# Performer stage: feature products by four heads, over 64 rows and 256 columns, in place of six heads over 96 rows and 384 columns

## The reference, cut to what matters

```
h   = layernorm(x) * g + b                        # 32 x 87 x 192
qkv = h as 12 heads of 16 channels                # queries, keys and values are the same
u   = (qkv / 16**0.25) @ proj.T                   # proj 64 x 16: 64 features a head
q_p = exp(u - diag - max over the features of u) + 1e-4
k_p = exp(u - diag - max over tokens and features of u) + 1e-4
out = (q_p @ (k_p.T @ qkv)) / (q_p @ sum over tokens of k_p)
x   = x + out
```

## Time and profile before

| | us |
|---|---|
| median of three runs | 2725.62 (2723.99 to 2726.18) |
| the profiled execution | 2753.35 |
| its span | 2751.6 |
| of it the stages: choosing, to about | 70 |
| the Performer stage, from the first product of features to the last row added | 78.4 to 349.3 |
| mean granted clock of TensorE | 0.752 of full |

### The profile page before, as it was taken

The page is one execution under the profiler, slowest core; times in us unless marked ns, Lnnn a source line. Parts: engine busy times, 40 slices in busy tenths (PEclk is TensorE's granted clock), DMA queues, the critical chain, the costliest instruction groups (busy, mean ns, idle before and its releaser), DMA issues. The chain is left out here.

```text
span 2751.6 us, 36305 instructions
## 1 busy us (share of the span) xinstructions
PE 1749.3 (64%) x11724; PEld 1429.1 (52%) x11724; DVE 1481.6 (54%) x2882; ACT 1128.2 (41%) x2242; POOL 333.7 (12%) x402
## 2 busy tenths in 40 slices
PE   3688869566413777645995623323966598429993
PEld 2466749365312444524892422222854498329993
DVE  6588841521277999675224599997143300562223
ACT  5366743212144687721123288872324054102220
POOL 0000000046300000000330000000000143013441
PEclk9688869789855888855996855555985599569996
DMA  3100000234400000003761000000020253316774
GB/s 81 54 17 16 21 10 1 73 87 128 137 6 3 6 6 3 2 9 102 227 194 53 3 6 5 5 1 0 1 67 18 80 183 125 119 48 220 223 222 140
DMA packets 135104, 185.74 MB, mean 68 GB/s; under 512 B 49248, under 2 KB 110115, under 8 KB 134803
## 3 DMA queue, kind: packets, MB, share of 16 engines
q1 hardware_dynamic: 117015, 146.70, 17.3%
q0 software_dynamic: 15360, 35.05, 4.6%
q10 hardware_dynamic: 2556, 1.77, 0.3%
HBM read 148.35 MB, written 32.96 MB: 66 GB/s over the span
## 5 line engine op out<-in xcount | busy, mean ns | idle before, releaser
L917 DVE TENSOR_TENSOR 49_l3f_mlp_hidden<-49_l3f_mlp_gate,49_l3f_mlp_first 128x512 f32<-128x512 f32 x51 | 35.1, 688 | 189.0 <-ACT 49_l3f_mlp_gate L898 165.3
L2054 PE MATMUL 14_pla_line<-14_pla_low,ident 128*128 128x435 f32 x96 | 68.0, 875 | 62.0 <-ACT 14_pla_low L2102 62.0
L813 PE MATMUL 49_l3f_mlp_first<-49_l3f_mlp_xT,49_l3f_mlp_w 128*128 128x128 f32 x816 | 101.1, 278 | 0.0
L2254 PE MATMUL 30_log_int_turned<-identb,30_log_int_ratio 128*87 128x128 bf16 x272 | 32.7, 315 | 107.3 <-DVE 30_log_int_ratio L2772 107.3
L1124 PE MATMUL 2_performer_p_u<-perf_proj,2_performer_yT 96*87 96x384 f32 x204 | 94.4, 613 | 9.2 <-DVE 2_performer_arg L1286 8.0
L813 PEld LDWEIGHTS 49_l3f_mlp_first<-49_l3f_mlp_xT,49_l3f_mlp_w 128*128 128x128 f32 x816 | 96.9, 195 | 0.0
L933 DVE TENSOR_SCALAR 9_l0f_mlp_y<-9_l0f_mlp_second,l0f_routing_weight 128x192 f32<-128x192 f32 x51 | 21.3, 418 | 138.9 <-PE 9_l0f_mlp_second L827 71.2
L898 ACT ACTIVATE 49_l3f_mlp_gate<-49_l3f_mlp_first 128x512 f32<-128x512 f32 x51 | 30.5, 598 | 134.8 <-PE 49_l3f_mlp_first L818 134.8
L2254 PEld LDWEIGHTS 30_log_int_turned<-identb,30_log_int_ratio 128*87 128x87 bf16 x272 | 29.2, 194 | 108.9 <-DVE 30_log_int_ratio L2772 108.9
L2265 PE MATMUL 30_log_int_p_out<-l2a_vb,30_log_int_wT 87*87 87x16 bf16 x384 | 30.9, 222 | 83.4 <-ACT 30_log_int_wT L2694 83.4
L931 DVE TENSOR_TENSOR 42_l3a_mlp_y<-42_l3a_mlp_second,l3a_experts_b_rows 128x192 f32<-128x192 f32 x29 | 10.4, 358 | 134.8 <-PE 42_l3a_mlp_second L827 115.5
(11 more groups left out here) (888 smaller groups left out, 5376.9 us busy)
## 6 DMA issues: line engine op xcount, KB each, us to landing
49_l3f_mlp_w<-in_L_ffn_w_dram SPq DMA_DIRECT2D x51, 768.0 KB
26_l1f_mlp_w<-in_L_ffn_w_dram SPq DMA_DIRECT2D x29, 768.0 KB
42_l3a_mlp_w<-in_L_attn_W_dram SPq DMA_DIRECT2D x29, 576.0 KB
9_l0f_mlp_w<-in_L_ffn_down_w_dram SPq DMA_DIRECT2D x102, 96.0 KB
l3a_experts_w<-in_L_attn_W_dram SPq DMA_DIRECT2D x8, 576.0 KB, 8.2
14_pla_blocks<-l1a_qkb SPq DMA_DIRECT2D x192, 5.4 KB, 1.8
l1f_experts_w<-in_L_ffn_w_dram SPq DMA_DIRECT2D x8, 384.0 KB, 6.6
30_log_int_blocks<-l2a_qkb SPq DMA_DIRECT2D x192, 5.4 KB, 1.8
```

Source lines behind the costliest of these rows:

```text
L813: nc.tensor.matmul(to(t + a * PAIRS), of[:, t + a * PAIRS, :], at[:, 0, :], start=(t == 0), stop=True, skip_group_check=True)
L917: v.tensor_tensor(hidden[j % 2][:], gate[j % 2][:], first[j % 2][1][:, 0, 0:HT, :], ALU.mult).then_inc(hidden_done, 1)
L2054: nc.tensor.matmul(to_w[:, n], kit.ident[:], of_w[:, n], start=start, stop=stop)
L2254: ins = nc.tensor.transpose(turned[:, n // 8, (n % 8) * 128:(n % 8 + 1) * 128], w[:, n * NT:(n + 1) * NT], kit.identb[:])
```

## The change

The heads are taken by four. `yT` has 128 rows: half k holds channels 64k to 64k + 127, so k = 0 holds heads 0 to 7 and k = 1 heads 4 to 11. `proj` has 128 rows and 256 columns: four heads block diagonally in rows 0 to 63, and the same again in rows 64 to 127. `features` computes three different products, each over 64 rows and 256 columns: heads 0 to 3 (lower rows, k = 0), heads 8 to 11 (upper rows, k = 1), heads 4 to 7 (lower rows, k = 1). No product is computed twice, but in block 4 all three are computed four times. In `p_u` heads 0 to 7 fill the first bank and heads 8 to 11 half of the second, and VectorE reads 768 values in one row. `proj` is loaded with eight DMAs in place of six.

```diff
-            for h in range(HEADS // 2):
-                sp.dma_start(proj[h * DH:(h + 1) * DH, h, :], dram["L0_attn_proj"]).then_inc(kit.arrived, 16)
+            for h in range(2 * QUAD):
+                sp.dma_start(proj[h * DH:(h + 1) * DH, h % QUAD, :], dram["L0_attn_proj"]).then_inc(kit.arrived, 16)
...
-            yT = several("yT", [KP, HALVES, NT], 2)
+            yT = several("yT", [TP, HALVES, NT], 2)
...
-            p_turn = kit.ps(ctx, "p_turn", [KP, 512])
+            p_turn = kit.ps(ctx, "p_turn", [TP, 512])
...
-            u_of = p_u[:, :, 0:HH * M].rearrange("t k (h m) -> t k h m", h=HH)
+            u_of = p_u[:].rearrange("t k w -> t (k w)")[:, 0:HEADS * M].rearrange("t (h m) -> t h m", h=HEADS)
...
-                        ins = t.transpose(p_turn[:, k * NT:(k + 1) * NT], Y[:, b, k * KP:(k + 1) * KP],
+                        ins = t.transpose(p_turn[:, k * NT:(k + 1) * NT], Y[:, b, k * 64:k * 64 + TP],
                                           kit.ident[0:NT, 0:NT])
...
                     again = 4 if b == 4 else 1
-                    for k in HALVES * again * [0] + [1]:
-                        ins = t.matmul(p_u[:, k, 0:HH * M], yT[b % 2][:, k, :], proj[:].rearrange("p h m -> p (h m)"),
+                    low, high = slice(0, 64), slice(64, TP)
+                    for rows, k, to in again * [(low, 0, p_u[:, 0, 0:QUAD * M]), (high, 1, p_u[:, 1, 0:QUAD * M]),
+                                                (low, 1, p_u[:, 0, QUAD * M:2 * QUAD * M])]:
+                        ins = t.matmul(to, yT[b % 2][rows, k, :], proj[rows].rearrange("p h m -> p (h m)"),
                                        start=True, stop=True)
...
-                    v.tensor_reduce(rmax[b % 2][:].rearrange("t (k h) -> t k h", k=2), u_of, AX.X,
-                                    ALU.max).then_inc(rmax_ready, 1)
+                    v.tensor_reduce(rmax[b % 2][:], u_of, AX.X, ALU.max).then_inc(rmax_ready, 1)
...
-            gb, proj = sb("perf_gb", [KP, 2, D], first), sb("perf_proj", [KP, HEADS // 2, 64], first)
+            gb, proj = sb("perf_gb", [KP, 2, D], first), sb("perf_proj", [TP, QUAD, 64], first)
```

More of the change, by code:

```diff
@@ L34 @@
 DH = D // HEADS
+QUAD = 4
 GB = 4
@@ L1285, in less_top @@
                         dve.wait_ge(ctx_done, b - 2)
-                    v.tensor_tensor(arg[b % 3][:, 0:HEADS * M].rearrange("t (k h m) -> t k h m", k=2, h=HH), u_of,
-                                    across(shift[b % 2][:].rearrange("t (k h) -> t k h", k=2), 3, M),
-                                    ALU.subtract).then_inc(less_ready, 1)
+                    v.tensor_tensor(arg[b % 3][:, 0:HEADS * M].rearrange("t (h m) -> t h m", h=HEADS), u_of,
+                                    across(shift[b % 2][:], 2, M), ALU.subtract).then_inc(less_ready, 1)
                 def find_rest(b):
@@ L2999, in build @@
             H0 = sb("H0", [NT, NB, D], first)
-            gb, proj = sb("perf_gb", [KP, 2, D], first), sb("perf_proj", [KP, HEADS // 2, 64], first)
+            gb, proj = sb("perf_gb", [KP, 2, D], first), sb("perf_proj", [TP, QUAD, 64], first)
             X1, Y = sb("l0a_x", [NT, NB, D], first), sb("perf_y", [NT, NB, D], first)
             choose_stage(kit, H0, X1, Y, gb, proj)
-            l0_attn(kit, H, X1, Y, stats, (gb, proj, (kit.arrived, 16 * (2 + HEADS // 2))))
+            l0_attn(kit, H, X1, Y, stats, (gb, proj, (kit.arrived, 16 * (2 + 2 * QUAD))))
         with ExitStack() as outer:
```

## The result

The median went from 2725.9 (2723.99 to 2729.1, four runs) to 2766.5 us (2765.37 to 2766.66, four runs): a ratio of 1.0147, 95% interval 1.0129 to 1.0164. So the kernel is 41 us slower, where 20 were forecast (2746, range 2703 to 2768). The direction holds, and the range holds the time by 1.5 us; the size is twice the forecast.

The account below looks back on a forecast made before the run. VectorE was taken to bound blocks at the high clock, TensorE at the low. Against the profiled 2753.35 us, +24.7 for low blocks, -7 start and +2 tail gave +20, 2773, carried to a median of 2746 us; range 2703 to 2768.

Parts of the forecast that it names:

- What bounds a block: Performer stage: VectorE bounds blocks at clock 1.00 (high, 6.02 us), TensorE those at 0.50 (low, 10.88 us before).
- The features: Six passes take the time of four as halves overlap: 1.79 us low for 3.84, 0.93 high for 1.94.
- Rival 3: The halves of the rows don't run side by side: 0.77 us more per low block, +59, 2785 us; chance 0.06.
- The low block: A block at clock 0.50 shortens by 2.05 us, from 10.88 to 8.83, with some 0.08 for edges.
- The count of low blocks: 20 of 26 blocks between 126 and 320 us stay at clock 0.50, 2.36 us each: 218.7 against 194, +24.7.
- rival 2: No clock rise, low throughout: +35, 2761 us; the far end of the forecast, with no chance of its own.
- Why none rose: Clock rises get rarer: the features' burst is halved, and for half of it only half the rows have work.
- rival 1: The clock behaves as before, so shorter features gain: -24 us, 2702; chance 0.17.
- The fall: The clock falls more easily: TensorE's idle time in a high block grows from 0.54 to about 1.5 of 6.00 us.
- The start: Up to block 5's features: -10 us from shorter features, +3 if the clock isn't up after block 4's burst; together -7.
- The tail: After block 31's features, high until 327.8 before: +3 us if the clock is low, taken at +2.
- The carry-over to the median: The profiled execution's 27.7 us above the median is carried over: 2773 us profiled becomes 2746.

Follow-up runs that it names:

- e2: The kernel before the change, with its repeated product of features computed once (block 4 as before), 96 rows; ratio 0.9994 to the kernel before.
- e3: The changed kernel with features over all 128 rows, in products of 256 and 512 columns, zeros in `proj` elsewhere; ratio 0.9902 to the kernel before the change.
- e12: The changed kernel with all three products over the lower rows, part of the result not computed; 2823.5 us against 2750.3 before the change, one execution each.
- e6: The changed kernel with unread products filling TensorE's idle places and block 4's repetition taken out; ratio 0.9997 to the kernel before the change.
- e9: The changed kernel with its three products in the order lower, lower, upper rows; ratio 1.0137 to the kernel before the change.
- e1: The changed kernel with its three products computed twice in every block; ratio 1.0028 to the kernel before the change.
- e10: e6 with three more unread products in each block from block 3 on; ratio 0.9881 to the kernel before the change.
- e5: The kernel before the change, with unread products filling TensorE's idle places and block 4's repetition taken out; ratio 0.9856 to the kernel before.
- e8: The changed kernel without an edit, measured again on another chip; 2795.0 us against 2754.5 before the change, ratio 1.0154.

## Why the prediction was right or wrong

**What bounds a block: right.** Low blocks follow TensorE: 10.88, 9.21 in the change, 9.61 in e2, 9.67 in e3, 10.06 in e12 move with the features, and with some 0.2 us around them where they run over 64 rows. High blocks stay VectorE's, 6.0 us (e6's line of 247 to 253).

**The features: right, with the account of the overlap wrong in its detail.** Forecast 1.79 and 0.93 us, measured 1.93 and 1.02. Rival 3 (no overlap, +59) fell: e12 shows what it would have been, 2.79 us and a stage 74 us longer than before. That four pass times are left of six holds; that it comes from the order of the passes does not (e9).

**The low block: mis-sized, by 0.38 us.** The term that was too small is the 0.08 for edges. Forecast 8.83, measured 9.21, which is 7.04 for the rest of the block, 1.71 for the passes and 0.46 for edges where I had put 0.08. The edges stand in three places: the features start 0.29 us behind the turning of the maxima (262.62 to 262.91) where it was 0.15, they take 1.93 for 1.71, and the transpositions behind the spread maxima begin 0.24 us after them (264.84 to 265.08) where it was 0.14. TensorE in order of time, before (beside 245.02 and 248.86) and after:

```profile
244.87 0.35 PE L1132 MATMUL 2_performer_p_top<-ident,2_performer_rmax 87*12 87x87 f32 x1
249.00 1.08 PE L1144 MATMUL 2_performer_p_qT<-ident,2_performer_arg 87*128 87x87 f32 x6
```

```profile
265.08 1.07 PE L1147 MATMUL 2_performer_p_qT<-ident,2_performer_arg 87*128 87x87 f32 x6
```

The prediction had the first and the last in view, found no gap that it could price, and left them out of the sum. The one within has nothing to do with the halves running side by side: it is as large in e12 (2.79 for six passes of 0.427). 26 blocks of 0.38 are 10 us. The Trainium skill (TensorEngine Tiling (Array Packing), Key Properties) says that a switch of the tiling mode drains the engine. The first and the last place (0.14 and 0.10) agree with it, and e2's block, without a switch, is 10.88 less 1.27, with no such edge; the 0.22 within, where all products are over 64 rows, is no such switch, and its cause is open. The range had 6 us for a low block that is 0.2 us longer; a step that is walked 26 times needed more room than that.

**The count of low blocks: mis-sized, and the main term.** I took 20 of 26, and all but block 5 were low. The six at 2.36 us are 14 us. 232.9 for all low, 9.9 more for the longer block, less some 2.5 for the high end of block 5 and for preparations that are hidden better, gives the 240.2 measured. VectorE's waits grew to 54.5 us where I had named some 45. The far end of the forecast, rival 2, was the case itself: +35 in its sum, +38.4 in the stage, and the difference is the edges less what the start gave.

**Why none rose: the reason was half right.** The prediction said that the run of features becomes too short, and that for half of it only half of the rows have work. The runs put the weight on the second. 2.6 us of 96 rows bring the clock back sometimes (e2, 0.69) and of 128 rows nearly always (e3, 0.89), while 2.8 us of 64 rows never did (e12, 0.50, one execution). Length does count at 64 rows: the run of e1, twice as long, took 0.50 to 0.77. Where I chose 20, I had no row that showed how often half the work on half the rows would do, and took a value inside the range that was nearer to what I knew. The rows that were there, a router at 5.89 of 6.00 and a low block at 10.54 of 10.90 that both stayed at 0.50, already said that something other than busy time decides.

**The rule on keeping busy: the trace decides against it as read.** The Trainium skill (TensorE: Matmul & The Clock Gate, What's actually happening) says that activity releases the throttle. By busy share, the kernel after was the more active one, 184.54 of 194 us for 170.31, and stayed at 0.50; e3 with 159.16 of 194 stood at 0.89. So rival 1, -24 us by that reading, fell.

**The fall: right in kind, not in the sum.** I expected falls to get easier, with TensorE idle for about 1.5 of 6.00 us in a high block (e6: 1.44), and put no term of its own on it. Since the clock never rose again, it didn't matter in the change itself. e6 and e10 show that it would have: 31 us between them.

**The start: better than the sum.** -10.6 for -7, since the clock did rise in block 4's burst of twelve 64-row products; I had this open between -7 and -10. **The tail:** +2.6 for +2.

**The carry-over to the median** was right: the stage's +38.4 is +41 in the medians. What lay 27.7 us above the median stood in a stage that the change doesn't touch; the prediction did not say where it stood, and its sum needed that.

The sum, put together: +20 forecast; +14 for the six further low blocks, +7 for the longer block with its offsets, -4 for the start, +1 for the tail give +38, against 38.4. That the range held is in part luck: it ends at 2768, and without the start's better 3.6 us the result would have lain above it.

## What to carry to other kernels

Before a product is shortened on an engine that waits anyway, ask what it does for TensorE's clock, and price the stage at both levels: here a set of features half as long cost 41 us, and one over all 128 rows, with zeros in `proj` for the heads that it doesn't need, gained 27 (e3). In this kernel the clock went with the rows that the products address, so try heads or zeros up to 128 rows before packing halves side by side, and put a few unread products where the engine runs dry beside another engine's long step (e5: 37 us from eleven places, with block 4's repetition taken out). And compare the stage, and not only two spans: two profiles differed by 29 us in a part that nobody touched.

## What the runs showed of the hardware

- The granted clock went with the rows at the same number of columns: 1536 columns a block gave 0.50 over 64 rows, 0.69 over 96 and 0.89 over 128 (0.50, 0.69 and 0.93 up to 280). Rows times columns alone don't order the kernels: e1 (3072 columns over 64 rows) and e3 (1536 over 128) are equal in it and stood at 0.71 and 0.93 up to 280. What share of this is rows with work and what share is rows addressed isn't separated: in all three a column of `proj` has 16 rows that aren't zero, and the turned tokens fill all the rows that are addressed. e3 also has another split of the columns (256 and 512, for 384 twice in e2); that was not tried by itself.
- An f32 product shows as two passes, and a pass of 384 columns takes 0.64 us at 1.2 GHz and 0.32 at 2.4 (3.84 and 1.94 us for six, and the earlier trace rows): 768 clocks, two a column.
- Two halves of the rows overlap whatever the order of the products (1.93 us in either order, 2.79 without the other half, at the low level).
- Features over 64 rows, between products over more of them, cost a block about 0.46 us more than their passes at the low level, in three places (0.14 ahead of them, 0.22 within, 0.10 behind).
- At the same work per block, the clock can fall in the midst of a regular rhythm (e6, at about 270) after it had held through several blocks of it. With three more small products in each block it did not fall from 130 to 316 (e10).
- The first expert stage took 123 us in one profile and 152 to 156 in the thirteen others, with the same products and the same bytes: its DMAs moved 156 GB/s in the one, and 126 in the profiles of before and of e8. What makes that difference was not tried.
